# Row scores of a causal attention contracted over 64 rows, two matmuls at a time in the array's two halves

## What is computed

```
q, k, v = split of hidden @ [Wq, Wk, Wv]      # 16 query heads, 4 key/value heads, 64 numbers a head
q, k = rope(q), rope(k)
scores = einsum("bkgqd,bkpd->bkgqp", q, k) * 64 ** -0.5     # 1024 x 1024 a head, causal
probs = softmax(where(causal, scores, -1e30))
out = probs @ v ; out @ Wo
```

## Time and profile before

| | |
|---|---|
| median of three runs | 2281.24 us (2279.39 to 2283.38) |
| profiled execution, its span | 2273.4 us; the median lies 7.8 us over it, which is the time around the program's first and last instruction |
| TensorE matmul busy | 1949.5 us, 86% |
| TensorE weight loads busy | 1718.9 us, 76% |
| VectorE busy | 1369.2 us, 60% |
| ScalarE busy | 854.9 us, 38% |
| GpSimd busy | 488.5 us, 21% |
| row scores, line 416 | 768 matmuls, 230.0 us busy |
| column scores, lines 433 and 434 | 768 each, 275.2 and 261.9 us |
| values, line 447 | 4608 matmuls, 538.4 us |
| row maxima, line 950 | 512, 373.0 us |
| waits of TensorE at line 416 | for the maxima 53.4 us in 176 places |

### The profile page before, as it was taken

How to read it: one execution, slowest core, us unless ns; L and a number is a source line. 1 busy time by engine, 2 the same in 40 slices (tenths; PEclk the granted TensorE clock), 3 DMA queues, 4 the chain that set the end, 5 groups by cost and what they waited for, 6 DMA issues and landing times.

```text
span 2273.4 us, 32271 instructions
## 1 busy us (share of the span) xinstructions
PE 1949.5 (86%) x11764; PEld 1718.9 (76%) x11764; DVE 1369.2 (60%) x3130; ACT 854.9 (38%) x1697; POOL 488.5 (21%) x940
## 2 busy tenths in 40 slices
PE   6858799999875789999976779999987587999997
PEld 4637699999744779999864569999976476999886
DVE  4688565463668755554358865555445885555535
ACT  1403444543331344445232334454423034444523
POOL 0231222121123212221023222112112322222111
PEclk8979799999987889999987879999998798999999
DMA  5400000000410000000050000000031000000005
GB/s 206 176 0 1 1 1 2 1 1 1 167 48 0 1 1 2 1 1 1 6 208 1 1 1 2 1 1 1 2 149 65 0 1 1 2 1 1 1 1 185
DMA packets 28526, 70.80 MB, mean 31 GB/s; under 512 B 4607, under 2 KB 19775, under 8 KB 24774
## 3 DMA queue, kind: packets, MB, share of 16 engines
q1 hardware_dynamic: 28358, 68.60, 8.2%
HBM read 58.35 MB, written 9.98 MB: 30 GB/s over the span
## 4 chain that ended last, share of the span: by engine, by line
PE 58%; DVE 22%; ACT 5%; DVEq 5%; issue 5%; DMA 2%; POOL 1%; SPq 0%; POOLq 0%; ACTq 0%
PE ps L447 20%; PE ps L293 7%; DVE ps L950 6%; PE ps L597 5%; PE ps L434 4%; PE ps L416 4%; PE ps L433 4%; PE ps L299 3%; DVE prod L1012 3%; PE ps L620 3%; PE ps L395 2%; ACT qhh L683 2%; DVE hrow L856 2%; DMA gate_scratch<-grow 1%; DVEq L1020 1%
## 5 line engine op out<-in xcount | busy, mean ns | idle before, releaser
L447 PEld LDWEIGHTS ps<-v,pT 128*128 128x128 f32 x4608 | 546.0, 192 | 12.5 <-ACT pT L700 2.0
L447 PE MATMUL ps<-v,pT 128*128 128x65 f32 x4608 | 538.4, 272 | 1.5 <-ACT pT L700 1.5
L700 ACT ACTIVATE pT<-ps 128x512 f32<-128x512 f32 (+3 forms) x768 | 332.9, 492 | 344.6 <-PE ps L434 332.4
L950 DVE CUSTOM_DVE_ANT_0 ps<-ps,mrow 128x128 f32<-128x128 f32 (+7 forms) x512 | 373.0, 783 | 40.2 <-PE ps L416 40.2
L1152 POOL TENSOR_SCALAR_AFFINE_SELECT pT<-pT 128x128 f32<-128x128 f32 x512 | 146.0, 294 | 928.5 <-ACT pT L700 922.8
L433 PE MATMUL ps<-qhh,khl 128*128 128x512 f32 (+3 forms) x768 | 275.2, 362 | 9.2 <-DMA q<-nmr 9.2
L434 PE MATMUL ps<-q,k 65*128 65x512 f32 (+3 forms) x768 | 261.9, 354 | 0.0
L416 PE MATMUL ps<-khl,qhh 128*128 128x512 f32 (+3 forms) x768 | 230.0, 381 | 35.5 <-DVE mx L950 15.0
L659 ACT ACTIVATE hfull<-ps,modb 128x512 f32<-128x512 f32 x48 | 37.3, 777 | 455.8 <-PE ps L371 455.8
L960 DVE RECIPROCAL den<-ps 128x4 f32<-128x4 f32 x128 | 23.4, 183 | 299.8 <-PE ps L447 299.8
L943 DVE TENSOR_TENSOR q<-ps,qhh 64x512 fp32r<-64x512 f32 x128 | 87.4, 683 | 185.8 <-ACT qhh L683 185.8
(11 more groups left out here) (150 smaller groups left out, 2897.1 us busy)
## 6 DMA issues: line engine op xcount, KB each, us to landing
sgn<-sgn_scratch SPq DMA_DIRECT2D x8, 1024.0 KB, 13.4
Kf<-kf_scratch SPq DMA_DIRECT2D x4, 2048.0 KB, 17.6
in_w<-in_w_scratch SPq DMA_DIRECT2D x4, 1536.0 KB, 10.7
x<-in_x SPq DMA_DIRECT2D x5, 1024.0 KB, 5.9
xn<-in_x SPq DMA_DIRECT2D x4, 1024.0 KB, 7.5
out<-x SPq DMA_DIRECT2D x4, 1024.0 KB, 5.0
wraw<-in_wmod SPq DMA_DIRECT2D x2, 1536.0 KB, 6.7
fwd<-in_fwd SPq DMA_DIRECT2D x5, 512.0 KB, 18.4
```

What stands on the lines that cost most here:

```text
L447: q = mm(ps[:, b, (i % 4) * (HD + 1):(i % 4 + 1) * (HD + 1)], pT[:, slot, i * P - lo:(i + 1) * P - lo], v1[:, g % 2, j, :], start=j == 0, ...
L700: A(pT[:, n % PRING, 0:(c + 1) * HALF - lo], ps[:, b, 0:(c + 1) * HALF - lo], ACT.Exp, scale=SCALE)\
L950: V.tensor_tensor_reduce(out=v, in0=v, in1=mrow[:, L - n:L], scale=1.0, scalar=-3e38, op0=ALU.add, op1=ALU.max, accum_out=mx[:, u % 2, i:i ...
```

## The change

Row scores leave out the product with k's remainder: they are q high times k high over 64 rows. One half of these matmuls takes rows 0 to 63 (qhh and khl), the other rows 64 to 127 (the second copy in qhh, and k2, whose rounded k moves there). Tiles 0 and 2 and the first 512 columns of tiles 4 to 7 use the upper half; tiles 1 and 3 and the columns over 512 use the lower. q2 and k2 grow from 65 to 128 partitions: row 0 has the negated maxima and the ones, rows 1 to 63 are filled with zeros, rows 64 to 127 have the remainder of q and the rounded k; so the second matmul of `score_cols` contracts over 128 rows. GpSimd fills k2 and q2 with three instructions where it had one, and the first DMA of the maxima waits for that (`sides_made`). On TensorE the row scores of head w stand in three bundles: tiles 0 to 3 before the values of tile 3, tiles 4 and 5 after the column scores 4 and 5, tiles 6 and 7 after the column scores 6 and 7.

```
-                q2 = sb("q2", [HD + 1, QRING, L], F32R, a3)
+                q2 = sb("q2", [P, QRING, L], F32R, a3)
-                k2 = sb("k2", [HD + 1, 2, L], F32R, a3)
+                k2 = sb("k2", [P, 2, L], F32R, a3)
@@ score_rows
-                    q = mm(ps[:, b + c // HALF, 0:e - c], qhh[:, r, i * P:(i + 1) * P], khl[:, g % 2, c:e],
-                           start=True, stop=True)
+                    if (i % 2 if n <= HALF else c // HALF) == 0:
+                        q = mm(ps[:, b + c // HALF, 0:e - c], qhh[0:HD, r, i * P:(i + 1) * P], khl[0:HD, g % 2, c:e],
+                               start=True, stop=True)
+                    else:
+                        q = mm(ps[:, b + c // HALF, 0:e - c], qhh[HD:P, r, i * P:(i + 1) * P], k2[HD:P, g % 2, c:e],
+                               start=True, stop=True)
@@ the order of a head on TensorE
                         if i == 3 and w < HEADS:
-                            for k in range(3):
+                            for k in range(4):
                                 score_rows(w, k)
                         q = values(u, 0, i, b)
                     q.then_inc(ready[b], 1)
-                    if w < HEADS:
-                        for k in range(3, 4):
-                            score_rows(w, k)
-                    for j in range(4, NT):
-                        score_cols(u, 1, j)
+                    for j in range(4, NT, 2):
+                        for k in range(j, j + 2):
+                            score_cols(u, 1, k)
                         if w < HEADS:
-                            score_rows(w, j)
+                            for k in range(j, j + 2):
+                                score_rows(w, k)
@@ ScalarE and VectorE, turn_head
-                        A(k2[0:HD, g % 2, cols], ps[0:HD, b, :], ACT.Copy).then_inc(s["k_done"], 1)
+                        A(k2[HD:P, g % 2, cols], ps[0:HD, b, :], ACT.Copy).then_inc(s["k_done"], 1)
-                    V.tensor_tensor(q2[0:HD, u % QRING, cols], ps[0:HD, b, :], qhh[0:HD, u % QRING, cols].bitcast(F32),
+                    V.tensor_tensor(q2[HD:P, u % QRING, cols], ps[0:HD, b, :], qhh[0:HD, u % QRING, cols].bitcast(F32),
@@ GpSimd
-                G.memset(k2[HD:HD + 1, :, :].bitcast(F32), 1.0)
+                G.memset(k2[0:HD, :, :].bitcast(F32), 0.0)
+                G.memset(q2[0:HD, :, :].bitcast(F32), 0.0)
+                pool.drain()
+                G.memset(k2[0:1, :, :].bitcast(F32), 1.0)
+                pool.drain().then_inc(s["sides_made"], 1)
                 pool.drain()
@@ SyncE
-                    dma(q2[HD:HD + 1, u % QRING, :].bitcast(F32), nmr[:, u % 2, :].bitcast(F32))\
+                    if u == 0:
+                        sp.wait_ge(s["sides_made"], 1)
+                    dma(q2[0:1, u % QRING, :].bitcast(F32), nmr[:, u % 2, :].bitcast(F32))\
```

More of the change, by code:

```diff
@@ L226, in adaln_hyena_binffn_gqa_moe @@
                  "q_done", "q_lo_done", "k_done", "k_lo_done", "nm_done", "nmr_done", "m_loaded0", "m_loaded1",
-                 "exp_done", "masked_done", "o_done", "oT_done", "top_done", "w1_loaded0", "w1_loaded1",
+                 "exp_done", "masked_done", "sides_made", "o_done", "oT_done", "top_done", "w1_loaded0", "w1_loaded1",
                  "expert_loaded0", "expert_loaded1", "egelu_done", "x_done"]
```

## The result

The changed kernel takes 2316.88 us (median of four runs, 2298.88 to 2333.86) against 2280.45 us beside it: ratio 1.013, 95% interval 1.0089 to 1.0172, slower. The median of 2316.88 is that of all four. The scatter is part of the finding: the kernel before spreads over 4 us in four runs, this one over 35.

A forecast was written before the change was run, and what follows sets the result against it. The prediction followed TensorE as the busiest engine, with VectorE's chain of maxima capping the gain. 14.3 us gained less 8.0 lost on fills made 6.3 us less: span 2267.1, plus 7.8 for the median, 2275 us; range 2257 to 2302.

The forecast's parts named there:

- The maxima on VectorE are the limit, 0.15 us behind: In 60 heads, faster row scores give at most 0.42 us each, 25 us, before VectorE's chain of maxima limits.
- The cost of a switch: Each entry to or exit from the 64-row arrangement costs 0.05 us; two of six per head precede the reciprocal, 0.10.
- The gain of pairs and order, 14.3 us: In the attention heads: 0.22 us gained in 48 heads and 0.31 in 12, together 14.3 us.
- The twelve heads for which I had 0.31: Heads that also turn keys: fourth tile costs about 0.06 us, only one switch counts, so 0.31 us gained each.
- Head 1, 0.22 like the others: Distance from head 0 to head 1: a gain of 0.22 us, as for the other plain heads.
- The fills, 8.0 us: Ahead of the first head, three GpSimd fills delay VectorE's normalising and TensorE's line 371 by about 2.0 us, four times.
- this does not come out; it turns into waiting: Attention heads: TensorE's own saving of some 0.8 us a head, 50 us in all, becomes waiting instead of gain.
- Rival 2, the array empties at every switch: Row-score switches cost d = 0.27 us each; 19 us lost, 27 with the fills: 2308 us, chance 0.27.
- Rival 3, no overlap: Row-score pairs don't run side by side; tile 3 adds 0.23 us, 7 us less gain: 2282 us, chance 0.10.
- Rivals 4 and 5: 4: the fills cost nothing, 2267 us, chance 0.13. 5: VectorE's chain is not the limit, 2255 us, chance 0.08.

The follow-up runs named there:

- e11: Kernel before, full height, old order except that row scores of tiles 6 and 7 follow column scores 6 and 7: 2258.3 us against 2278.8, ratio 0.992.
- e4: Changed kernel with row scores over 128 rows in heads 0, 4, 8 and 12: 2278.6 us against 2276.5 for the kernel before, ratio 1.0006.
- e8: Kernel before with its one fill of k2 made three times on GpSimd: 2289.9 us against 2278.8, ratio 1.0051.
- e2: Changed kernel with all row scores in the upper half, no two side by side: 2336.6 us against 2276.5 for the kernel before, ratio 1.0258.
- e12: Kernel before with the new TensorE order and 64 rows only in the first bundle of heads 0, 4, 8, 12: 2279.9 us against 2275.4, ratio 1.0022.
- e10: Changed kernel with tiles 4 to 7 over 128 rows in heads 0, 4, 8, 12: 2291.2 us against 2277.4 for the kernel before, ratio 1.0065.
- e3: Changed kernel with the three fills moved behind the first rotations on GpSimd: 2283.4 us against 2276.5 for the kernel before, ratio 1.0014.
- e5: Changed kernel with the old TensorE order, six separate row-score places a head: 2428.1 us against 2278.8 for the kernel before, ratio 1.0659.

## Why the prediction was wrong

I forecast 2275 us with 2302 as the upper end; it is 2317.

- **The maxima on VectorE are the limit, 0.15 us behind.** Right: line 427 trails line 958 by 0.15 in the heads at full clock, and e11 shows the full 0.42.
- **The cost of a switch.** Mis-sized. From the last value to the first row score pass 0.20 us where it was 0.08, so 0.12 to get in; after the last pair the values start 0.11 late. I took 0.05 from the change of columns, and that row was no model for a change of rows. But weights for the two halves are loaded together (both first loads start at 378.12), which I did not see; the reciprocal comes only 0.17 late after the first row score, where tile 3 and one way out were to make 0.15.
- **The gain of pairs and order, 14.3 us.** Mis-sized: the 14 distances behind head 1, for which I had 13.4 us in sum, give 4.7 (e4). After its first row score a plain head has line 958 done 0.22 us later than before (7.30 for 7.08): 0.17 from the reciprocal, and the rest behind it, where the maximum of tile 4 starts 0.71 after that of tile 3 instead of 0.61; its scores, which I had ready at 2.8, end at 2.96. That leaves 0.20 of the 0.42. The way in stands ahead of the first row score and takes another part, so that a plain head gains 0.10 to 0.15 in place of 0.22. The twelve heads for which I had 0.31 gain 0.15, and the twelve longest distances lose. I had taken one timeline for all heads.
- **Head 1, 0.22 like the others.** It gains 1.4 in each element, 5.6 in all, by a shorter time at clock 0.50. That e4's sum of 10.3 comes as near to 14.3 as it does is luck.
- **The fills, 8.0 us.** The mechanism was right to the row (6.2 us forecast, 6.23 measured; the projection behind comes 2.1 later for 2.0), the term too small: 11.0 in the trace, 11.1 in e8. The missing 0.7 each time is TensorE's own: the projection lasts 6.79 us for 6.04, longer at clock 0.50. My upper end was 11.
- **No term for the clock.** This is the step that failed. I wrote of the time saved on TensorE that "this does not come out; it turns into waiting", and let the stage go on at clock 1.00 as in the rows, whatever stands in it; 64 rows were to cost the switches and nothing else. The rows showed the place, a key-turning head in which TensorE waits inside the first bundle, and I used it only for its length. With 64-row matmuls in that bundle the clock drops to 1.2 GHz: 53 of the 59 us of the profiled execution. No rival of mine had it. It isn't the saved time that does it: e2 and e12 save no columns, and the clock falls there too.
- **Rival 2, the array empties at every switch.** The right side for the wrong reason: 0.12 and 0.11, not 0.27. The Trainium skill (TensorEngine Tiling (Array Packing), Key Properties) says that a change of the tiling mode drains the engine; for 128 to 64 rows the traces agree with a small price, for 128 to 64 columns shows 0.05 at the most.
- **Rival 3, no overlap.** Refuted by the start times and by e2. **Rivals 4 and 5** fell with e8 and with line 427, 0.15 us behind the maxima.

With the measured terms: 10 less for the heads, 11 more for the fills, and some 36 for the falls of the clock, which is the remainder of the median and not measured by itself (53 in the slowest run, the profiled one). Without the falls it is e4, no change that can be told.

## What to carry to other kernels

Before making matmuls cheaper in a stage whose limit is elsewhere, ask what clock it will be granted with them, and read it from the trace place by place: half-height matmuls in heads where TensorE also waits inside the bundle turned a neutral change into a loss of 1.3% and a scatter of 35 us. Keep them out of such a place (four matmuls in four of sixteen heads were enough), and bundle them, since every way in and out costs 0.2 us or more. Before you credit a gain to a change, see whether it lies where the clock differs: more than half of what e4 gains in its heads does. And read which bank each take waits for: moving one pair of row scores behind a pair of column scores gave more than the tiling could.

## What the runs showed that I had not expected

- A stretch at 1.2 GHz lasts 3.4 us where full-height matmuls follow (e10), 6.8 in e12, 20.5 where pairs follow (changed kernel, e3, e5) and 23.9 where single 64-row matmuls follow (e2). What a fall costs goes with what is issued after it. Why 6.8 in e12 and 3.4 in e10, with full height behind both, stays open.
- The same kernel seems to have a different number of such stretches in each run, though only one run of each has a trace: ten runs of e3 lie between 2268.4 us (mean granted clock 0.929) and 2302.5 (0.916), and the four of the changed kernel stand in order of their clocks, 2298.9 at 0.919 to 2333.9 at 0.896.
- VectorE gets one instruction through per fill on GpSimd, and one that has started 0.16 us before a fill is still held to its end: the first of the four takes 2.1 us, from 236.37 to 238.48. In e3, with the same fill of v1 just ahead of it and no other fill beside it, it takes 0.41.
